# A decoder on one core: new lane orders and counts of filling products in the middle stage, another lane order in the last stage

## The reference

```python
# the rest of L0_ffn: down projection of the quantised hidden part
x = _layernorm(x + _L0_ffn_ref(x, ...))
# L1_attn: attention in segments of 64 tokens, plus attention to
# every fourth token of the neighbour segments (1 and 2 away)
x = _layernorm(x + _L1_attn_ref(x, ...))
# L1_xattn: 16 heads of 64 features against 64 context tokens
k, v = jnp.split(image @ Wkv, 2, axis=-1)
attn = jax.nn.softmax(jnp.where(mask, q @ k.T * scale, mask_value))
x = _layernorm(x + (attn @ v) @ Wout + bout)
```

## Time and profile before

| what | us |
|---|---|
| median of three runs (lowest, highest) | 3060.8 (3058.64, 3072.15) |
| the profiled execution's own time | 3052.98 |
| its span, first to last instruction | 3051.2 |
| middle stage, first `product` to last far part | about 348 to 1226 |
| last stage | 1501 to 3051 |

### The profile page before, as it was taken

How to read it: one execution, slowest core, us unless ns; L and a number is a source line. 1 busy time by engine, 2 the same in 40 slices (tenths; PEclk the granted TensorE clock), 3 DMA queues, 4 the chain that set the end, 5 groups by cost and what they waited for, 6 DMA issues and landing times.

```text
span 3051.2 us, 49389 instructions
## 1 busy us (share of the span) xinstructions
PE 2415.3 (79%) x21152; PEld 1644.0 (54%) x21152; DVE 1689.6 (55%) x4103; ACT 1041.1 (34%) x1536; POOL 357.5 (12%) x605
## 2 busy tenths in 40 slices
...
GB/s 90 1 1 3 1 1 9 1 8 8 9 1 8 8 8 1 103 40 94 165 1 1 1 8 1 1 1 1 8 1 1 1 1 4 4 1 1 1 1 28
DMA packets 39341, 47.91 MB, mean 16 GB/s; under 512 B 7169, under 2 KB 36369, under 8 KB 38354
## 3 DMA queue, kind: packets, MB, share of 16 engines
...
## 4 chain that ended last, share of the span: by engine, by line
PE 58%; DVE 24%; ACT 9%; issue 4%; POOL 4%; DMA 1%; SPq 0%; DVEq 0%; ACTq 0%; POOLq 0%
PE banks L2608 7%; DVE wide_area L2481 4%; PE banks L1487 3%; PE banks L2805 2%; DVE wide_area L1891 2%; PE banks L2355 2%; PE banks L1452 2%; PE banks L1518 2%; PE banks L920 2%; PE banks L2364 2%; PE banks L1799 2%; PE banks L2595 2%; PE banks L2374 2%; PE banks L1784 2%; PE banks L948 2%
## 5 line engine op out<-in xcount | busy, mean ns | idle before, releaser
L2481 DVE TENSOR_REDUCE wide_area<-banks 128x8 f32<-128x2048 f32 x64 | 146.7, 2292 | 118.8 <-PE banks L2355 118.7
L2805 PE MATMUL banks<-wA 128*128 128x128 f32 x1290 | 192.2, 297 | 6.0 <-DVE spread L1406 6.0
L2805 PEld LDWEIGHTS banks<-wA 128*128 128x128 f32 x1290 | 171.9, 208 | 16.0 <-issue 8.7
L2460 ACT ACTIVATE weights<-banks 128x2048 f32<-128x2048 f32 x64 | 120.1, 1877 | 132.5 <-PE banks L2364 132.5
L1007 POOL TENSOR_TENSOR rstd<-moments,eps 128x4 f32<-128x4 f32 x56 | 11.9, 212 | 1213.7 <-DVE moments L996 1213.7
L991 DVE BATCH_NORM_STATS2 stats<-banks 128x6 f32<-128x128 f32 x208 | 50.2, 287 | 177.9 <-PE banks L959 108.1
L1891 DVE TENSOR_REDUCE wide_area<-banks 128x16 f32<-128x1024 f32 x80 | 94.3, 1218 | 38.6 <-PE banks L1784 38.0
L2268 DVE TENSOR_TENSOR weights<-banks,wC 128x1024 f32<-128x1024 f32 x64 | 76.8, 1217 | 23.0 <-PE banks L2131 22.6
L1487 PE MATMUL banks<-gates,wide_area 128*128 128x128 f32 x512 | 87.3, 322 | 0.0
L1000 DVE TENSOR_SCALAR xs<-banks,moments,rstd 128x128 f32<-128x128 f32 x208 | 70.6, 402 | 29.8 <-POOL rstd L1009 29.4
L2608 PE MATMUL banks<-wide_area,big 128*128 128x512 f32 x192 | 86.8, 593 | 0.0
...
## 6 DMA issues: line engine op xcount, KB each, us to landing
...
```

The costliest lines, as they stand in the source:

```text
L2460: act.activation(m.weights, bank[:, :, :].rearrange("p r c -> p (r c)"), ACT.Exp, scale=DK ** -0.5)\
L2481: return dve.tensor_reduce(m.peaks[:, k % 2, :, :].rearrange("p t (r c) -> p r t c", r=4)[:, :, :, SPARE[j]], m.bank[:, :, :].rearrange("p ...
L2805: pe.matmul(bank[:, 0:P], m.ident, m.ident, start=True, stop=True)
```

## The change

It edits two tables and nothing else: BUSY and ORDERS (parts "alone", "middle", "closing" and "last"). The work done and its results are the same.

```diff
-BUSY = {'lead z': 2, 'lead norm': 10, 'lead product': 10, 'back0': 4, 'back1': 1, 'dil_scores0': 1, 'dil_turned0': 2, 'dil_sum0': 2, 'dil_scores1': 3, 'dil_turned1': 1, 'dil_sum1': 2, 'near norm': 14, 'first3': 3, 'far norm': 1, 'gate': 5, ...}
+BUSY = {'lead z': 3, 'lead norm': 6, 'lead product': 14, 'out0': 1, 'back0': 5, 'scores1': 1, 'dil_turned0': 2, 'dil_sum0': 2, 'dil_scores1': 1, 'dil_turned1': 4, 'dil_sum1': 2, 'near norm': 12, 'wide start': 1, 'wide out2': 1, 'first3': 6, 'far norm': 4, 'gate': 3, ...}
     "alone": {
-        "pe": "nnffnnfnnnnnnnnnnfffnnnfnnnnnnnnnnnnnn",
-        "dve": "nfnnfnnnnnfffffnnnnnnnnnnnnnnnnn",
-        "act": "nnnnnnnnnnnnnnnnnnnfffffnnfnnn",
+        "pe": "nnffnnfnnnnnnnnnnffffnnnnnnnnnnnnnnnnn",
+        "dve": "nfnnfnnnnnffffnnnfnnnnnnnnnnnnnn",
+        "act": "nnnnnnnnnnfffffnnnnfnnnnnnnnnn",
     "middle": {
-        "pe": "nffnfnfnfnnnfnffnfnfnnfnfnfnnfnnfffffnnfffnnfnnfffnnnfnnnn",
-        "dve": "nffnfnffnnnffnfnfffnnnfnnffffffnnfffnnfnfffffnnnnnnn",
-        "act": "fnffnnnfnfffffnnnnnffffnnnnffffffnnnnnnnfffffffnnn",
+        "pe": "nffnfnfnfnnnfnffnfnfnnfnfnfnnfnnfffffnnfffnnfnnffffnnnnnnn",
+        "dve": "nffnfnffnnnffnfnfffnnnfnnffffffnnfffnnnffffffnnnnnnn",
+        "act": "fnfffnnnnfffffnnnnnffffnnnnffffffnnnnnnnfffffffnnn",
     "closing": {
-        "pe": "nffnfnfnfnnnfnfnfnffnnfnfnfnfnnnfffnnfnnnnfnnnnnnn",
-        "dve": "nffnfnffnnnfnfnffffnnnfnnffffffnnnnnnnnnfnnfn",
-        "act": "fnffnnnfnfffffnnnnnffffnnnnnnffffnnnnnffnnn",
+        "pe": "nffnfnfnfnnnnffnnffnnfnfnfnfnfnnfffnnnnfnnfnnnnnnn",
+        "dve": "nffnfnffnnnfnnffffnnnfnfnffffffnnnnnnnfnnnnfn",
+        "act": "fnfffnnnnfffnnnnffnffffnnnnnnfffnnnfnnffnnn",
...
     "last": {
...
```

More of the change, by code:

```diff
@@ L792 @@
 SPARE_PAIR = {0: 16, 1: 17, 2: 0, 3: 1}
-BUSY = {'lead z': 2, 'lead norm': 10, 'lead product': 10, 'back0': 4, 'back1': 1, 'dil_scores0': 1, 'dil_turned0': 2, 'dil_sum0': 2, 'dil_scores1': 3, 'dil_turned1': 1, 'dil_sum1': 2, 'near norm': 14, 'first3': 3, 'far norm': 1, 'gate': 5, 'taken': 20, 'chosen': 5, 'choice start': 8, 'choice same': 4, 'choice bit': 3, 'choice rank': 40}
+BUSY = {'lead z': 3, 'lead norm': 6, 'lead product': 14, 'out0': 1, 'back0': 5, 'scores1': 1, 'dil_turned0': 2, 'dil_sum0': 2, 'dil_scores1': 1, 'dil_turned1': 4, 'dil_sum1': 2, 'near norm': 12, 'wide start': 1, 'wide out2': 1, 'first3': 6, 'far norm': 4, 'gate': 3, 'taken': 20, 'chosen': 5, 'choice start': 8, 'choice same': 4, 'choice bit': 3, 'choice rank': 40}
 ORDERS = {
@@ L830 @@
     "last": {
[L831 to L860, removed]
@@ L861 @@
-        "pool": "fnnfnnffnnnnnnnnnnnnffffffffffffnnnnffffnnnfffnnnnnnnnnnnnnnnnffffffffffffffffnnnnnnnnnnnnnnffffffffffffffnnnnnnnnnnnnnn"
+        "pe": "nnffnnnfnnnnnffffffnfnnfnnfnffnfnfnnnfnnffnffnffffnnnnnnnnnnffffnfffffffnnnnnnnnnfffnfffffffnnfnfnfnfnffnnfffffnfnnffnff"
+             "nnnnfnnffnffnnfnfnnnnnnffnnfnnnffffffnfnfnnnfnfffnfnnfnnfnnfnfnfffffnnnnnnnffffnfffnfnfnfnfnfnfnfnfnfnfnfnfnfnfnfnfnfnfn"
+             "fnfnfnnfnfnfnfnfnfnfnfnnffnnnnfnnnfnfffffffnnnnnnnnfnnnfffffffffffnnnnnnnnnnnnfffffnnnnnnnnnnfffnnnnffffffnfnfnffnnnfnnf"
+             "nfnfnnnnnffffnffnfnffnfnnffnnfnnffnnnnfnnnfnnnnfffnnnnnnnnnfnfnnffnfnffnfnfnnnnfffnffffffffnnnfffffnfffnnfnnfnnnfnfffnfn"
+             "nfffnnnnnnnfffnfnffnnfnffnfffnnnnnnfffnnfnffnnnnnnnfffffnffnnffnnfffnfnfnfnfffnfffnfnfffnffffnfnfnfnfnnfnfnfnfnfnfnfnfnf"
+             "nfnfnfffnfnnnfnnnfnnnnffnnnnfnfnnnnfnfnfffffffnnnnnffffffnnfnnnfffffffnnfnnfffnnnnffffffnnnnffnnnnffffffnnffffffffnfffnn"
+             "fffnnnnfffnnffffnfnnfnfnfffnfnnnfnnnnfnnnnfnfffnnfnnfnnnfnnnnfffnfnnfffnfnfnffnnnnffffffffnffnnfnfnfnnffnfffnnnfnfnffnnf"
+             "nnfnnffnnnnnffnnnnnfffnnfnnnnffffffnnfnnnfnnnffnfnnnfnnnnfnffnfnfnfnffnfnffnfnffnnffffnfnffnfnfnfnfnfnfnfnfnfnnfnfnfnfnf"
+             "nfnnffnnnnfnnnnnfnfnnnnnnnfnnnnfffffnnnnnnfnnnnnnnnnnnnnnnnffnnnnnnffnnnfnfnfnnffffffnfnnfffnnfnffffnfffnnnnnnnnffffffnf"
+             "fnnnnfnfnnfffnfffnnnfffffnnnnnfnnnnfffnfnnffnnfffnnnnfffffnnnfnffnnfnfnnfnfnfnfnfnfnfffnfnnffffnnfffffffnnnnnffffffnfffn"
+             "fffnnffnfffnfffffnfffffnffnfnnfnnfnffnffffnnnnnnffnfnffnnfnfnffnffnfnfnffffnfnffnnfffffffnfnfnfnfnfnfnfnfnfnfnfnfnfnfnfn"
+             "fnfnffnnnffnnnnffnnnffnnnnnnnnfnfnnffffffnnnnnffnffnnnfnffnfnnffffnnfffffffnnnnfffffnfnffffffffnffffffffnnnnffff",
@@ new lines @@
+        "dve": "nnffnnnfffnnfnnfnfffnnnnnnffffffnnnnnnfffnfffnfnfnnfnnnffnfffnnfnfffnnffnnfffnnffffnfnnffnnnnffnfnfnfnnnfnnffnnnfnnffffn"
+             "nfnfffnnnnnfffnfffnnnnnnnfffffnfffnnfnffnnffnnffnnffnnffnnffnnffnnffnnnnnffnfnfnffffnnnnnnnnffnfffnfffnnfnnnnnffffnnnnnn"
+             "nnnfnfffnnnnnffnfffffnnnnnnnffnfnnnnnnfffnffnnnfnnfffffnnffnnffnffnfffnnffnnfnnnnfnnnffnnfnnnfnfnfnnfnfffffnnnffnnffnfff"
+             "nnnfnnnfnfnfffnfnfnffnfffnfffnfffffnfffnfnffnnffnnffnnffnfnfnnnnfnnfnnffnnnnnfnnnfnffffffnfnfnnfffffffffnnnnffffnnfffnnf"
+             "nnnfffffnnfnffffnnnnnfffnfffnnnnnnnnnfffnnnffnfnfnffnnfnffffnnfffnfnnffnnnffnfnnnfnfnnffnnnnfnfnfnnnfnnffnnfnfffnnnfnfnf"
+             "ffnffnnnnnnnffnfnnnffffffnnfffffnffnfnfnffnnffnnffnnffnnfnnnnfnnnnfnnnfnnnnnfnfnnnnnnnnffnnnnnnnfffffnnfnffnnnnnffffnfff"
+             "fnnnnnfnnnffnffnnnnnnffnnffnnnfffffnnffnnffnnfnnnnfffnffnnfnnnnfffnffnffnnfnfffnfnfffnnffnfffnnnfffnnfffffffnfffffffnnnf"
+             "nnfnnfffnfnfnnfffnfffnfffnnffffffffnfnffnnffnnffnnffnnffnnnfnfnnnnffnnnnffnnnnfnfnfnffnnffffffffffffffffnnnnffff",
```

15 lines of the change are left out of this document (13 added, 2 removed).

## The result

The changed kernel took 3018.15 us in the median of four runs (3009.62 to 3032.19), against 3060.2 for the kernel before beside it: a ratio of 0.9858, with a 95% interval from 0.9826 to 0.989. So it is faster, by 42 us or 1.4 per cent (34 to 53 us by the interval), where 34.6 us were forecast. The profiled execution was the slowest of the four, 3032.19 us with a span of 3030.4.

A forecast was written before the change was run, and what follows sets the result against it. No engine is full, so TensorE's waits count. 7 x (5.7 - 0.9) = 33.6, plus 1 for the start, is 34.6 us: 3053.0 becomes 3018.4, and the median's 7.8 above gives 3026; range 3008 to 3047.

The forecast's parts named there:

- The forecast case: Whole kernel: the summed gain of 34.6 us holds, giving 3026 us; chance 0.72.
- 1, ScalarE's copies: Ahead of far's scores0: copying w0 before near's exponentials ends TensorE's wait and clock fall; 5.7 us per pass gained.
- 2, the counts: Filling products, 61 to 68 per pass: some lie on the path, costing 0.9 us per pass, bounds 0 and 1.6.
- 3, lead's moves: Lead's resid behind near's queries, its features ahead of near's dil_sum1: 0, bounds -0.3 and +0.4 us per pass.
- 4, alone and closing: First near part: 1 us less, bounds -4 and +3; closing pass: 0 beside the copies' gain, bounds -3 and +3.
- 5, the last stage: 417 of 1216 TensorE steps change place; either sign equally likely, so 0, bounds 12 us to each side.
- Rival C: Last stage: its new order is better as well, by 5 us per round, giving 3006 us; chance 0.08.
- The sign that I had named: Last stage: within 1538 to 1562 us if right, over 12 us from 1550 if wrong.
- A: Passes: idle time goes but the clock still falls once per pass elsewhere; gain 15, so 3045 us; chance 0.11.
- B: Last stage, self attention: 64 units each pay one more wait, 67 us in all, giving 3093 us; chance 0.04.
- D: Wait at L1483: VectorE's w1 or GpSimd's mask causes it, so moving copies does nothing; 3066 us; chance 0.02.

The follow-up runs named there:

- experiment 1: Kernel before, with only ScalarE's copies w00 and w01 moved ahead of near's exponentials in the middle and closing passes: 3017.64 us, ratio 0.9888.
- experiment 3: Changed kernel with the old counts of filling products (61 per pass), new orders everywhere: 3002.27 us, ratio 0.9852.
- experiment 7: Kernel before, with the new order of the last stage alone: 3049.88 us, ratio 0.9957.
- experiment 10: Two reruns on one chip: changed kernel with old counts, 3017.99 us; changed kernel with few filling products in the six middle passes, 3004.7 us.
- experiment 6: Changed kernel with the old order of the last stage: 3036.07 us, ratio 0.9898.
- experiment 5: Changed kernel run again without an edit, as a base on the chip of other runs: 3023.85 us, ratio 0.9863.
- experiment 2: Kernel before, with thirteen filling products in the idle time ahead of far's scores0, ScalarE's old order kept: 3035.2 us, ratio 0.9948.
- experiment 9: Kernel before with six, then three filling products ahead of far's scores0; no whole times given, passes 98.6 to 100.2 and 100.2 to 101.6 us.
- experiment 4: Changed kernel with ScalarE's old order restored in the middle and closing passes (w00, w01 behind near's exponentials): 3044.65 us, ratio 0.9986.

## Why the prediction was right, point by point

The forecast case came true in its main term; 3018.15 lies in the range, 8 below the value. One term, the last stage, was put at 0 and came to 10 to 13 us. That this lies at the edge of its bounds of 12 is no merit of its reasoning, which had no row for it.

**1, ScalarE's copies: right in mechanism and size.** Predicted 5.7 us per pass with the products of `out0` and `back0` in it. The swap alone gave 6.48 against the profile of before (experiment 1). Those products took 0.69 back (`scores1` 28.03 us after near's queries in experiments 1 and 3; 28.83 in the changed kernel, 0.11 of the difference being `wide start`'s), so 5.8. Against the profile of experiment 7, whose passes are 0.7 us shorter with the same code, the two figures are 5.8 and 5.1. In the pass of the earlier trace rows `scores1` was forecast at 28.7 us after near's queries and came at 28.83.

**2, the counts: right in sum, two places off.** Beside `out0` and `back0` they cost 0.74 us a pass, 0.9 was predicted. `first3` pushed near's turned maxima back by 0.62 (0.66 predicted), near's `scores1` by 0.20 (0.22). `wide start` cost 0.11 in place of 0.22, since q5 and q6 wait for copies anyway, and `lead z` nothing, since near's `dil_out1` behind it follows from the turned scores. Lead's `product` was only just hidden: it ends at 716.02, VectorE's maximum at 716.04, and near's turned maxima start at 716.10. What I had not seen is the other side: in the closing pass, without lead's work, the counts keep the clock up and are worth 5.4 us. I had put that pass down at part 1 and the counts alone (4.8 less). It came out at 5.7 less than in the profile of before, but by another way: with the old counts, the new orders and the swap it takes 106.7 and 106.6 (experiments 3 and 10), where the code of before took 107.0 in one profile and 104.1 in another. So in this pass the swap and the orders show no gain, and the counts carry it.

**3, lead's moves:** 0.11 us per pass for the orders together (95.54 against 95.43); bounds were -0.3 and +0.4.

**4, alone and closing:** the first near part, near's queries to near's queries, was 86.9 to 89.0 us with the old counts and 86.0 to 87.6 with the new. In the profiles of before and after it grew from 86.95 to 87.6, where 1 less was forecast; within the bounds.

**5, the last stage: the step that failed.** "With both signs equally likely, I take 0" was wrong by 10 to 13 us: 12.2 by experiment 6, 13 by experiment 7, 8 to 10 in TensorE's idle time. The price that I used, the commonest wait (L2417), hardly moved (48 waits and 50.8 us, 46 and 48.8). The gain is the balance of many smaller places: TensorE's wait ahead of the cross attention's turned maxima (L1791 on VectorE's maximum L1891, 21.3 to 17.8) shrank, others shrank by 1 to 3 us, and at least one grew (L1808 on L1853, 4.8 to 10.4). Which of the moves made which wait shorter was not tested. It stood at the edge of my bounds. Rival C had the sign, but its size of 20 was too large. The sign that I had named, the last stage within 12 us of 1550, could not tell: to the end of the span the stage took 1555.1 us in the profile of the changed kernel and 1529.9 in its second one (experiment 5).

**The sum:** 29.6 + 5.7 + 0.7 = 36.0 for everything up to the end of the middle stage, in the traces, against 34.6 forecast. Against the profile of experiment 7 the same stretch, first near part to last far part, is 873.2 less 841.5, so 31.7. With 10 to 13 for the last stage this makes 42 to 49; 42 was measured, with an interval of 34 to 53 us.

**The rivals.** A (the clock falls all the same) is refuted by experiments 1 and 2: the six passes of experiment 1 are at 1.00. Its core, that a fall can come elsewhere, is true of the closing pass, and the reason that I gave against it (waits of 0.7 to 0.9 us did not bring the clock down) holds for the profile of before only: in experiments 2, 7 and 9 the clock fell once behind a gap of 0.94. B (last stage worse by 67) is refuted by experiments 6 and 7, D (another wait behind L1483) by experiments 1 and 4.
